# Sorting graph edges: the edge attributes come in whole 21-word record rows, laid out by partition on the host

## The reference

```python
edge_index = jnp.stack([src, dst])
x = _layernorm(x + _L0_gnn_ref(x, src, dst, edge_type_8, ...))
# layer 1: a weight matrix for each edge, made from the edge's attributes
w = (efeat @ We + be).reshape(-1, IN_FEATS, OUT_FEATS)
m = jnp.einsum('ei,eio->eo', feat[src], w)
neigh = jax.ops.segment_sum(m, dst, num_segments=num_nodes)
...
x = _layernorm(x + _L2_gnn_ref(x, ..., edge_index, edge_type_8))
x = _layernorm(x + _L3_gnn_ref(x, edge_index, ...))
```

## Time and profile before

| | us |
|---|---|
| median of 3 runs | 16680.38 |
| lowest and highest run | 16605.38, 16702.47 |
| span of the profiled execution, first to last instruction | 16996.1 |
| the span's part up to 300 (constants, zeroed tables) | 300 |
| of it the sort, from 300 to 6870 | 6570 |
| of it the four layers behind | 10126 |

### The profile page before, as it was taken

The page is one execution under the profiler, slowest core; times in us unless marked ns, Lnnn a source line. Parts: engine busy times, 40 slices in busy tenths (PEclk is TensorE's granted clock), DMA queues, the critical chain, the costliest instruction groups (busy, mean ns, idle before and its releaser), DMA issues. The chain is left out here.

```text
span 16996.1 us, 429738 instructions
## 1 busy us (share of the span) xinstructions
PE 11995.3 (71%) x146289; PEld 8312.1 (49%) x146290; DVE 10824.2 (64%) x19718; ACT 8088.7 (48%) x16130; POOL 5158.9 (30%) x4771
## 2 busy tenths in 40 slices
PE   1343443434434344799799998997996999999998
PEld 0111111111111111466688886665664888888887
DVE  3233333333333333688788887887886899999998
ACT  1232433433424234566466664665664555555554
POOL 1656666565664656000111111000000111111111
PEclk8555555555555555899899998999998999999999
DMA  7122222222222222688222222887885222333322
GB/s 208 48 72 59 81 67 66 81 59 71 74 58 79 58 72 82 184 229 229 89 106 106 106 106 95 234 235 198 235 235 126 80 83 83 85 85 84 84 84 71
DMA packets 1721891, 1905.31 MB, mean 112 GB/s; under 512 B 981549, under 2 KB 1429103, under 8 KB 1696207
## 3 DMA queue, kind: packets, MB, share of 16 engines
q1 hardware_dynamic: 1602775, 1863.79, 37.0%
q0 software_dynamic: 116864, 39.75, 1.5%
q10 hardware_dynamic: 2078, 0.15, 0.0%
HBM read 1449.57 MB, written 453.42 MB: 112 GB/s over the span
## 5 line engine op out<-in xcount | busy, mean ns | idle before, releaser
L688 POOL DMA_INDIRECT rec<-sort_ring,sort_idx x3520 | 4042.6, 1148 | 2791.9 <-issue 1469.7
L1381 DVE TENSOR_TENSOR e_full<-e_feats,e_masks 128x3840 bf16<-128x3840 bf16 x1179 | 2523.7, 2154 | 350.5 <-ACT e_feats L1339 302.0
L1294 PE MATMUL e_acc<-e_full,e_sel 128*128 128x384 bf16 (+1 forms) x11760 | 2120.9, 327 | 270.4 <-DVE e_full L1381 270.2
L778 PE MATMUL sort_ps_count<-sort_hot,upper_b 128*128 x400 | 231.6, 579 | 2689.9 <-DVE sort_hot L903 2144.6
L1530 PE MATMUL e_acc<-e_outer,e_sel 128*128 128x272 f32 x7840 | 1896.8, 397 | 3.9 <-DVE e_outer L1625 3.9
L1337 ACT CAST e_masks<-e_kind 128x1280 bf16<-128x1280 fp8e4 x1179 | 1482.6, 1258 | 629.5 <-DVE e_full L1381 575.0
L731 ACT CAST sort_cols_t<-sort_ps_late 120x256 f16<-120x256 f32 x98 | 39.5, 403 | 3439.8 <-remote 2373.0
L1530 PEld LDWEIGHTS e_acc<-e_outer,e_sel 128*128 128x128 f32 x7840 | 1459.2, 190 | 281.2 <-issue 4.1
L953 DVE TENSOR_TENSOR sort_over<-sort_ps_late,sort_late_base 128x20 f32<-128x20 f32 x175 | 30.7, 176 | 2428.1 <-remote 2208.7
L1294 PEld LDWEIGHTS e_acc<-e_full,e_sel 128*128 128x128 fp8e4 x11760 | 1061.0, 97 | 933.2 <-issue 298.1
L751 ACT ACTIVATE sort_made<-sort_ps_count,sort_window_bias 128x1024 fp8e4<-128x1024 f32 (+1 forms) x1274 | 1378.7, 1156 | 71.9 <-remote 26.7
(11 more groups left out here) (463 smaller groups left out, 22855.8 us busy)
## 6 DMA issues: line engine op xcount, KB each, us to landing
e_hot<-stream SPq DMA_DIRECT2D x888, 480.0 KB, 3.8
stream<-sort_made SPq DMA_DIRECT2D x98, 2568.0 KB
e_sel<-stream SPq DMA_DIRECT2D x1176, 160.0 KB, 2.7
e_st<-stream SPq DMA_DIRECT2D x99, 1888.0 KB, 7.3
sheaf_gather<-stream SPq DMA_DIRECT2D x393, 384.0 KB, 3.1
e_hot<-stream SPq DMA_DIRECT2D x294, 448.0 KB, 3.5
tail<-sort_made SPq DMA_DIRECT2D x98, 660.0 KB
sheaf_by_dst<-tail SPq DMA_DIRECT2D x491, 128.0 KB, 3.0
```

What stands on the lines that cost most here:

```text
L688: nc.gpsimd.indirect_dma_start(out=rec[q], out_offset=bass.IndirectOffsetOnAxis(ap=idx[:, s, q, c:c + 1], axis=0), in_=ring[:, s, q, c, :] ...
L1294: last = mm(acc[h][:, 0:cols_all], now[:, n * P:(n + 1) * P], full[q & 1][:, n, :], start=j == 0, stop=j == NT - 1)
L1381: v.tensor_tensor(full[q & 1][:, :, 0:cols].rearrange("p j (t k f) -> p j t k f", t=TYPES, k=3), feats[q & 1][:, :, :, :].unsqueeze(2).to_ ...
```

## The change

The host no longer passes the attributes as `[edges, 16]`. It pads each edge to 21 words and lays the array out as `[128, tiles, 21]`, so that for one partition the five tiles of a step stand behind each other, in the ring's own form. A transfer now carries whole records, 5 x 21 words for each partition, attributes and five words of zeros; the ones and the fields have to be written after it. So ACT waits for `attr_in` in each step, copies 20 ones (from a column of `iota` that holds 1) and then the four fields. POOL's own wait for `attr_in` goes, since the fields now come behind the attributes. In `pads`, ACT writes the ones alone.

```diff
 def load_attrs(n):
@@
-    sp.dma_start(ring[:, place_of(i), q, :, 0:D].squeeze(1),
-                 edges[:, tiles(t0[q] + local(i, i0) * C, C), :]).then_inc(attr_in, 16)
+    sp.dma_start(ring[:, place_of(i), q, :, :].squeeze(1),
+                 attr[:, tiles(t0[q] + local(i, i0) * C, C), :]).then_inc(attr_in, 16)
@@ pool
     pool.wait_ge(fields_ready, u + s + 1)
     pool.sem_inc(passed, 1)
-    pool.wait_ge(attr_in, u * (16 * Q) + (s + 1) * (16 * Q))
-    pool.sem_inc(passed, 1)
     pool.wait_ge(idx_ready, u + s + 1)
@@ scalar
+    ones = m.iota[:, 1:2].unsqueeze(1).to_broadcast([P, Q, C])
@@ prepare
     with act.Fori(i0, i1) as i:
+        act.wait_ge(attr_in, i * (16 * Q) + 16 * Q)
+        act.sem_inc(act_passed, 1)
+        nc.scalar.copy(ring[:, place_of(i), :, :, D:D + 1].squeeze(1).squeeze(3), ones)
         for q in range(Q):
@@ pads
     with act.Fori(i0, i1) as i:
-        act.wait_ge(scattered, i + 1)
-        nc.scalar.copy(ring[:, place_of(i), 0, :, D + 1:D + 5].squeeze(1), e.fields[:, 0:C, :]).then_inc(fields_ready, 1)
+        act.wait_ge(attr_in, i * (16 * Q) + 16 * Q)
+        act.sem_inc(act_passed, 1)
+        nc.scalar.copy(ring[:, place_of(i), :, :, D:D + 1].squeeze(1).squeeze(3), ones).then_inc(fields_ready, 1)
@@ host
-    host["attr"] = np.pad(attr, ((0, ATTR_TILES * P - N_EDGES), (0, 0)))
+    attr = np.pad(attr, ((0, ATTR_TILES * P - N_EDGES), (0, RW - D)))
+    host["attr"] = np.ascontiguousarray(attr.reshape(ATTR_TILES, P, RW).transpose(1, 0, 2))
```

More of the change, by code:

```diff
@@ L587, in _ @@
             def _(sp):
-                edges = attr.rearrange("(t p) f -> p t f", p=P)
                 def load_attrs(n):
@@ L657, in _ @@
                     for q in range(Q):
-                        sp.dma_start(ring[:, place_of(i), q, :, 0:D].squeeze(1), edges[:, 0:C, :]).then_inc(attr_in, 16)
+                        sp.dma_start(ring[:, place_of(i), q, :, :].squeeze(1), attr[:, 0:C, :]).then_inc(attr_in, 16)
                 move_blocks(QUADS - 1, BLOCKS - (QUADS - 1) * Q)
```

## The result

| | before | after |
|---|---|---|
| median of 20 runs each, us | 16658.80 (16589.40 to 16718.74) | 16733.74 (16670.91 to 16805.21) |
| ratio, 95% interval | | 1.0047, 1.0032 to 1.0063 |
| profiled execution, its span | shown ahead of the prediction | 16805.21, 16803.4 |

The change made the kernel 0.47% slower, 75 us, where I had forecast 15750. The two profiled executions differ by more than the kernels do: 181.9 us of span, where the medians differ by 75.

A forecast was written before the change was run, and what follows sets the result against it. POOL's scatters, dry at quad starts because increments came late, were taken as the limit: 1251 - 167 = 1084 us off 16996 gives 15912, or 15596 if the 316 are spread; middle 15750, range 15450 to 16600 with 0.80.

The forecast's parts named there:

- What bounds the kernel: In the sort, POOL runs dry at quad starts because idx is late, DVE's L953 waiting for late TensorE increments; 1265.7 us.
- The step that failed: In the sort, bursts of 64-byte attribute packets were read as the source of late increments and SP's slow issues.
- rival 1: Late increments come from POOL's scatters or TensorE, or timed runs hardly have them; nothing gained, 16680 us, chance 0.13.
- Transfers: Attribute transfers in the sort: 4 x 128 pieces a step for 4 x 640; quad packets from 25145 to about 10800.
- SP: SP's 28 transfer issues of a quad: some 34 us in place of 91.81.
- DVE: DVE's seven steps of a quad end at about 3153, not 3253; L953's wait under 500 us.
- POOL: POOL's scatters become the bound; removing its waits for idx gives back 1251 us.
- The slower scatters beside DVE's tables: POOL's scatters slow while DVE makes a quad's fourth block tables, no longer in idle time; costs 167 us.
- ACT's wait in order: At quad starts, ACT's attribute wait delays next keys by 5 us (3.8 to 13.8); 115 us, hidden if POOL is bound.
- rival 3: If DVE's increment delays stay, ACT's later keys cost 5 us at 23 quad starts; slower, 16795 us, chance 0.07.
- The 316 us between span and median: Median of before lies 316 us below the profiled span; if in these waits, forecast 15912, if spread, 15596.
- The rule against it: Skill's rule: large descriptors matter only when DMA engines or the issuing sequencer bind; the change buys nothing, 16680 us.

The follow-up runs named there:

- quarter_scatter: Kernel before with one scatter in four, only the first block's records of each quad written; 14246.53 us in a single run.
- pause_3: Kernel before with three fills of an unused tile ahead of each of POOL's steps, pausing its scatters; 16410.92 us, ratio 0.9635.
- before_again: Kernel before, unchanged, profiled a second time for a profile nearer its median; span 16621.5 us.
- after_pause_3: Changed kernel with three fills of an unused tile ahead of each of POOL's steps; 16385.38 us, ratio 0.9691 to the kernel before.
- pause_3_again: Kernel before with three fills ahead of each of POOL's steps, timed again in a later group; 16422.29 us, ratio 0.9714.
- keys_first_again: Changed kernel with ACT making the next step's keys before its wait for the attributes, second timing; 17120.26 us, ratio 1.0051 to the kernel before.
- after_again: Changed kernel as it is, timed again in a later group; 17062.89 us, ratio 1.0025 to the kernel before.
- acts_only: Kernel before with only ACT's and POOL's part of the change, transfers still 640 pieces of 64 bytes; 17075.99 us, ratio 0.9983.
- no_loads: Kernel before without attribute transfers in the sort, SP incrementing their semaphore itself; 16818.19 us, ratio 1.0107.
- after_pause_2: Changed kernel with two fills of an unused tile ahead of each of POOL's steps; 16273.15 us, ratio 0.9579 to the kernel before.
- late_twice: Kernel before with TensorE's six matmuls for the late rows issued twice in each step; 17254.82 us, ratio 1.0383.
- late_two: Kernel before with two matmuls for the late rows per step instead of six, DVE first summing earlier tiles; 17295.48 us, ratio 1.0104.
- both_two: Kernel before with four matmuls per step for twelve, late rows and main count, DVE summing earlier tiles; 17890.23 us, ratio 1.0443.

## Why the prediction was wrong

*What bounds the kernel:* right up to the increments. POOL dry at the quads' starts, because `idx` is late, because L953 waits: when the pauses freed L953, exactly those waits went.

***The step that failed*** is the one sentence "that it comes from the attribute packets is my reading, from their number, and because SP's slow issues and TensorE's late increments both appear between 3110 and 3140". What the runs showed in its place: both are held back by POOL's scatters. With a quarter of the scatters L953 never waits and SP's issues take 32.57 us; with no attribute transfers L953 waits as before. As I read it now, the two appear together because a quad's steps begin there. The row that spoke against it was in the prediction, under rival 1: the last wait of a quad comes 50 us after the last attribute packet. I explained it away as a backlog. Its counter-argument, that SP has no part in scatters, was no argument: the hold isn't limited to engines that share work.

*Transfers:* 10905 packets in a quad for 10800 forecast. Right, and worth nothing.

*SP:* 75.26 us for 28 issues, 34 forecast. Wrong, by the same step; the 32.57 of quarter_scatter are what it takes unhindered.

*DVE:* the forecast for L953 was under 500 us. It was 2063.3.

*POOL:* the 1251 us stayed out with the step above. The slower scatters beside DVE's tables, minus 167, didn't show either: where POOL did become the bound (pause_3), its scatters took 3982.6 us, not more than the 4042.6 of the earlier trace rows. Nor were the 1265.7 us typical, as 763.9 in `before_again` show.

*ACT's wait in order:* 5 us at each of 23 quad heads, range 3.8 to 13.8, from rival 3. The head grew by 4.29 us (16.41 less 12.12), 99 us in 23 quads; the kernel lost 75. The wait itself was sized right, and so was the condition: where POOL is the bound (after_pause_3 against pause_3_again, runs of 16377 to 16393 against 16410 to 16426), the cost is hidden, and the change is even 0.2% faster. But keys_first_again, with the head restored, was no faster than after_again. As long as the increments are late, a quad's length isn't a sum: 4 us earlier in one place come back as a wait in another. So the 4.29 us are where the loss shows, and not shown to be its cause. acts_only, the half that has ACT's wait and the same long heads, showed no loss (0.9983, 0.9958 to 1.0007), and no_loads, without ACT's wait, lost 1.07%. That the loss came out near rival 3's size is therefore luck as far as these runs tell. What would fit all four is that SP's transfers, when they are quicker, let POOL scatter sooner in a quad, with fewer gaps that free the increments. That is argued from the pauses' result; no run tested it alone, and what the 0.47% are made of stays open.

*The 316 us between span and median:* I let them decide between 15912 and 15596. Between the two profiles of before, 342 of the 375 us lie in the sort (its last scatter ends at 6838 and at 6496), and there L953 and `idx` differ by 223 and 502 us: the first of my two cases. Times like that span are also what this kernel takes in the median in the four later groups.

*The rule against it* was the better forecast. The Trainium skill (Perfetto Trace Analysis, What "DMA-bound" means) makes large descriptors matter only where DMA engines or the issuing sequencer bind. With DMA at 0.22 in the sort of after, the trace agrees.

The outcome is rival 1's cause, which had 0.13, and a loss near the size of rival 3's, which had 0.07. Rival 1 named POOL's scatters as a possible source. I gave it little because "they should be 1084 us under the span" if the timed runs had no such waits, which argued only against runs without waits, not against rival 1.

## What to carry to other kernels

When an increment arrives long after the instruction that makes it, look for what was running all through the delay and not for what began beside it; take that away, and take the suspect away, before changing either for good. Two such experiments here (no_loads, quarter_scatter) settled the matter. And where one engine streams small indirect DMAs while others do many small instructions, try a pause in the busy engine. Here 175 gaps of 3.4 us, 595 us in all, came with a time that was 729 us shorter (16273.15 for 17001.8).

## What the runs showed of the hardware

- While POOL issues scatters one each 1.27 us (0.96 and 0.30), increments of other engines come up to 43 us late; the first steps after a rest go at full pace, and a gap of 3.4 us or more behind each 25 us of scatters kept the waits under 26 us (25.7 at the longest in after_pause_2, 15.9 in pause_3).
- The longest delay grew by 2.4 us for each small matmul more (late_twice) and fell by 2.6 for each one less (late_two), though TensorE's rows have each done in 0.17 us.
- It isn't bound to one engine: it showed on SP, whose 28 issues took 75 to 92 us in place of 32.57, and on DVE in both_two, whose waits for its own increments grew from 0.2 to 3 us. I had expected a hold on one engine.
- In both_two TensorE's granted clock in the sort was 1.00 (2.4 GHz), 0.53 in `before_again`, and yet the profile gives the same 480-column matmul 593 ns in both_two and 582 in `before_again`. (The ends of matmuls are modelled in this profile.)

One candidate for the mechanism stands in the Trainium skill (NOTIFIC — the notification-queue block, Constraints, capacities, measured rates, and Overflow: three behaviours, one of which stalls the engine): the block that writes an execution's records can take about 500 of them in flight, and holds back their producers beyond that. A stretch at full pace and then a hold that ends in a gap would look like it, though 40 of the 71 long waits of `before_again` end without a gap. Against it stand the layers: there TensorE alone ran 13.7 matmuls in a us (135490 in 9900 us), each with its record, for 1.7 in the sort's stretch (10714 in 6400), and no wait of the layers in `before_again` ends with "remote". No run here shows or excludes it, since all executions were taken with their records; one without was not tried.
